# Who subtracts the attention's complement counts, and when their products run: one change to a graph network kernel on one core

## What is computed

```python
x = (meta_x @ W).reshape(N, HEADS, DIM)
a_src = jnp.sum(x * att_src, axis=-1)
a_dst = jnp.sum(x * att_dst, axis=-1)
logits = a_src[src] + a_dst[dst]
logits = jax.nn.leaky_relu(logits, NEG_SLOPE)        # slope 0.2
seg_max = jax.ops.segment_max(logits, dst, num_segments=N)
ex = jnp.exp(logits - seg_max[dst])
seg_sum = jax.ops.segment_sum(ex, dst, num_segments=N)
alpha = ex / (seg_sum[dst] + 1e-16)
msg = x[src] * alpha[:, :, None]
out = jax.ops.segment_sum(msg, dst, num_segments=N)
return out.mean(axis=1) + bias
```

## Time and profile before

| | |
|---|---|
| median of 3 runs | 1313.79 us (1310.27 to 1314.24) |
| the profiled execution | 1312.94 us, of which the span from first to last instruction is 1311.0 us |
| granted clock, mean of the span | 0.884 |
| busy over the span | PE 1171.5 us (89%), PEld 1106.4 (84%), DVE 884.3 (67%), ACT 624.2 (48%), POOL 63.0 (5%) |
| the 20 attention blocks, first nadS copy to last eviction | 855 us to 1303 us |

### The profile page before, as it was taken

One profiled execution on the slowest core, in us unless ns is written; L12 is line 12 of the kernel. 1 busy time (PEld: TensorE's weight loads), 2 busy tenths in 40 slices (PEclk: granted clock), 3 DMA queues, 4 the chain that ended last, 5 costly groups with the idle time before them and its releaser, 6 DMA issues.

```text
span 1311.0 us, 41073 instructions
## 1 busy us (share of the span) xinstructions
PE 1171.5 (89%) x17195; PEld 1106.4 (84%) x17195; DVE 884.3 (67%) x2404; ACT 624.2 (48%) x1143; POOL 63.0 (5%) x113
## 2 busy tenths in 40 slices
PE   0688888888999999999998699499999999999996
PEld 0588888888999999999986699488888888887996
DVE  1899999996443443443732723679778878887887
ACT  0566666662000000000112101478788888888886
POOL 2000000001111111111000001000000000000000
PEclk9855555558999999999999699699999999999998
DMA  1544444430000000000000000000000000000000
GB/s 27 83 70 60 63 65 68 63 58 11 3 3 2 3 2 2 3 2 2 3 2 2 1 2 2 1 2 1 2 1 2 2 1 2 2 2 1 7 12 12
DMA packets 133692, 21.47 MB, mean 16 GB/s; under 512 B 132961, under 2 KB 133378, under 8 KB 133538
## 3 DMA queue, kind: packets, MB, share of 16 engines
q1 hardware_dynamic: 132190, 18.75, 9.6%
q10 hardware_dynamic: 1252, 0.31, 0.1%
q0 software_dynamic: 96, 0.16, 0.1%
HBM read 18.41 MB, written 0.80 MB: 15 GB/s over the span
## 4 chain that ended last, share of the span: by engine, by line
PE 66%; DVE 17%; ACT 9%; issue 5%; DMA 1%; SPq 1%; POOL 0%; ACTq 0%; DVEq 0%; POOLq 0%
PE bank L1655 34%; PE bank L1781 11%; PE bank L1566 7%; PE bank L1777 5%; ACT Mr L852 4%; DVE Mr L1427 3%; PE bank L1569 3%; DVE ohk L941 2%; DVE ohp L943 2%; DVE Mr L1434 1%; ACT eahl L675 1%; PE bank L1570 1%; PE bank L1772 1%; ACT F L815 1%; DVE F L1326 1%
## 5 line engine op out<-in xcount | busy, mean ns | idle before, releaser
L1655 PEld LDWEIGHTS bank<-GH,C 128*128 128x128 f16 x8025 | 451.6, 98 | 8.3 <-issue 5.1
L1655 PE MATMUL bank<-GH,C 128*128 128x128 f16 x8025 | 453.7, 220 | 4.3 <-DVE GH L995 4.3
L1781 PE MATMUL bank<-F,Mr 128*128 128x260 f16 (+1 forms) x2520 | 343.7, 268 | 7.6 <-DVE Mr L1427 4.0
L852 ACT ACTIVATE Mr<-eaT 128x640 f16<-128x640 f32 x433 | 326.6, 822 | 30.1 <-PE bank L1781 28.1
L1781 PEld LDWEIGHTS bank<-F,Mr 128*128 128x128 f16 x2520 | 218.8, 98 | 31.1 <-DVE Mr L1427 4.7
L1427 DVE TENSOR_TENSOR Mr<-Mr,C 128x640 f16<-128x640 f16 x433 | 195.7, 488 | 72.7 <-ACT Mr L852 71.0
L725 ACT ACTIVATE plo<-bank 128x256 f32<-128x256 f32 (+1 forms) x91 | 32.8, 360 | 400.2 <-PE bank L1655 389.9
L1777 PE MATMUL bank<-FN,C 128*128 128x130 f16 x2260 | 209.8, 220 | 0.9 <-DVE r L1335 0.9
L1100 DVE TENSOR_TENSOR S<-bank,plo 128x256 f32<-128x256 f32 (+1 forms) x91 | 36.0, 395 | 246.9 <-ACT plo L725 246.9
L1566 PE MATMUL bank<-ohk,ohp 128*128 128x100 f16 (+3 forms) x1452 | 168.7, 281 | 10.8 <-DVE ohp L943 10.3
L1777 PEld LDWEIGHTS bank<-FN,C 128*128 128x128 f16 x2260 | 164.1, 98 | 10.5 <-DVE r L1335 1.4
(11 more groups left out here) (229 smaller groups left out, 834.7 us busy)
## 6 DMA issues: line engine op xcount, KB each, us to landing
raw<-in_edges_dram SPq DMA_DIRECT2D x242, 68.0 KB, 2.1
xs<-in_x_dram SPq DMA_DIRECT2D x1, 800.0 KB, 4.5
out_dram<-xs SPq DMA_DIRECT2D x4, 160.0 KB
wg<-in_L_gnn_W_dram ACTq DMA_DIRECT2D x2, 64.0 KB
z<-in_L_gnn_att_src_dram SPq DMA_DIRECT2D x1, 128.0 KB, 2.9
z<-in_L_gnn_att_dst_dram SPq DMA_DIRECT2D x1, 128.0 KB, 3.9
out_dram<-xs SPq DMA_DIRECT2D x1, 128.0 KB
wts<-in_L_gnn_W_dram ACTq DMA_DIRECT2D x3, 16.0 KB
```

Source lines behind the costliest of these rows:

```text
L852: act.activation(Mr[:, mi % RB, :], nadS, ACT.Sigmoid, bias=steep[:, h, t:t + 1], scale=-STEEP / XS).then_inc(s_step, 1)
L1655: last = pe.matmul(bank[:, b, jj * 2 * D:(jj + 1) * 2 * D], C[:, t, (t0 + jj) * P:(t0 + jj + 1) * P], GH[:, par, t, :], start=t == 0 and j ...
L1781: return pe.matmul(bank[:, k, a_:z_], Mr[:, mi % RB, j * P:(j + 1) * P], F[:, t, a_:z_], start=start, stop=t == T - 1)
```

## The change

The rule `apart` now takes the units 0, 4, 8, 12, 16 and 20 of blocks 1, 2 and 3, in all four heads: 72 units. Before it took these six in blocks 1 and 2 and four (0, 7, 14, 21) in block 3, in the first three heads: 48 units. GpSimd forms all complements, in a stream of its own that waits for the mask (`s_M`) and for the buffer (`s_Nu`). VectorE's `complement` is gone. PE takes the products of a complement after the masked products three units later, not one.

```diff
-            return h < H - 1 and (b in (1, 2) and t % 4 == 0 and t < T - 1 or b == 3 and t % 7 == 0)
+            return b in (1, 2, 3) and t % 4 == 0 and t < T - 1
...
-            with pool.If(dense3 == 0):
+            with pool.If(dense3 == 1):
+
+                for (h, b, t), ni in APART.items():
+                    pool.wait_ge(s_M, unit(h, b, t) + 1)
+                    if ni >= RN:
+                        pool.wait_ge(s_Nu, ni - RN + 1)
+                    pool.tensor_tensor(Nr[:, ni % RN], Mr[:, unit(h, b, t) % RB, :], C[:, t, b * NT * P:(b + 1) * NT * P], ALU.subtract).then_inc(s_N, 1)
+            with pool.Else():
...
-                            if t and apart(h, b, t - 1):
-                                complement(h, b, t - 1)
...
-                            if t and apart(h, b, t - 1):
-                                ni = APART[h, b, t - 1]
+                            if t >= 3 and apart(h, b, t - 3):
+                                ni = APART[h, b, t - 3]
                                 pe.wait_ge(s_N, ni + 1)
                                 for j in range(NT):
-                                    last = pe.matmul(bank[:, BANKS[b][j], 2 * S1:4 * S1], Nr[:, ni % RN, j * P:(j + 1) * P], F[:, t - 1, 2 * S1:4 * S1], start=False, stop=False)
+                                    last = pe.matmul(bank[:, BANKS[b][j], 2 * S1:4 * S1], Nr[:, ni % RN, j * P:(j + 1) * P], F[:, t - 3, 2 * S1:4 * S1], start=False, stop=False)
```

More of the change, by code:

```diff
@@ L1381, in final @@
                         last.then_inc(s_fin, 1)
[L1383 to L1389, removed]
                 scaled(0, 0)
```

## The result

The changed kernel takes 1366.43 us (median of 4 runs, 1361.57 to 1368.66) against 1313.76 for the kernel before: ratio 1.0402, 95% interval 1.0367 to 1.0436. It is 52.7 us slower; 1370 was forecast, inside 1316 to 1440. The profiled execution took 1368.66 us, its span 1366.8, 55.8 us longer than before's.

The account below looks back on a forecast made before the run. PE and VectorE were taken as level in blocks 1 and 2 of the first three heads. GpSimd's exclusions add 30 us there, 11 in blocks 3, 17 in the last head: + 58 on 1312.94, forecast 1370 us, range 1316 to 1440.

Parts of the forecast that it names:

- What bounds the kernel: Blocks 1 and 2 of the first three heads: PE and VectorE level, about 0.4 us of VectorE slack a block.
- the slack: VectorE's spare time in each of three last-head blocks, beyond its forced wait at the start: 1.0 us.
- What is removed: VectorE loses 48 complements of 0.40 us, 19 us in all; PE loses 6.7 us, 5.0 of them in the last head.
- rival 1: Faster: no exclusion between 16-bit masks and GpSimd, PE's 6.7 us gained; about 1306 us, 1302 to 1310; chance 0.13.
- The instruction's length: Each of 72 GpSimd complements of 640 16-bit elements takes 1.52 us, scaled by elements from 32-bit rows.
- The exclusion: GpSimd's complements and VectorE's two-tile masks exclude each other in full, costing VectorE 1.3 us each.
- rival 2: GpSimd goes by bytes, 0.85 us an instruction, one exclusion 0.65 us; + 13, 1326 us; chance 0.10.
- The new waits: PE's wait for a complement three units on should be free; ScalarE's wait for `s_N` is covered by 1.6 us of masks.
- a sign that it was wrong: In the changed profile, VectorE waiting for sigmoids in the middle of blocks would speak for starved GpSimd.
- Work under which GpSimd hides: GpSimd runs 1.5 us under two `scaled` in each block 3, and 1.0 us under pieces of `final` in last-head blocks.
- rival 3: GpSimd gets in only when masks run out; VectorE stands 2.2 us, not 1.3, 72 times; 1435 us; chance 0.10.
- rival 4: The clock falls as PE gets gaps of about 1.3 us; + 170, 1540 us; chance 0.05.

Follow-up runs that it names:

- the fills: Changed kernel with GpSimd filling the buffer twice in place of each complement: 1319.92 us; with a second complement buffer as well, 1310.48 us.
- the two runs that differ only in the engine: Changed kernel with a second complement buffer, once with VectorE forming all 72 complements, 1317.63 us, once with GpSimd forming them, 1360.76 us.
- the run with the engine alone: Kernel before, with GpSimd instead of VectorE forming its 48 complements; same units, products one unit behind, one buffer: 1343.10 us, ratio 1.0226.

## Why the prediction was right, point by point

- **What bounds the kernel**: right for blocks 1 to 3 of the first heads; two engines were level, and VectorE's time reached the end. For the last head the slack was wrong. I took 21.59 - 18.08 - 2.5 = 1.0 us for VectorE; six complements of 0.40 us on VectorE cost 1.9 to 2.1 of their 2.4 us there, so it was 0.3 to 0.5. The trace of before shows where the 1.0 us went. Its waits between 1234.06 and 1255.65 (total, times, longest) are:

```profile
DVE Mr L1427 <- ACT Mr L852: 3.1, 4, 2.4
```

  That is 0.6 us more than the 2.5 that I took off, for the second, third and fourth mask, and the 0.4 us that are left are, in VectorE's timeline, gaps of some 0.03 us between the small instructions of `post` and `final`, each of which waits for the one before. Idle time counted in a block is not all free.
- **What is removed**: right. 0.40 us each on VectorE. PE's 6.7 us came to nothing, as said, since PE was no longer the bound. But with the stops taken away (the fills, two buffers) the last head still didn't give PE's 1.7 us a block, as VectorE was level with PE there too, so rival 1 at 1306 was too low even if its mechanism had held: the fills ended at 1310 with two buffers and at 1320 with one.
- **The instruction's length**: 1.52 us forecast, 1.39 measured alone and 1.57 as the median, where it waits for a running mask. The error was small because the 32-bit rows carried over by elements; 0.60 us for 320 elements is 1.9 ns an element.
- **The exclusion**: right in kind. The 16-bit pair, which no row had shown, excludes like the others, so rival 1 is out, and so is rival 2, by the instruction's length. By the forecast's own rule, 1.39 - 0.28 + 0.08 = 1.19 us, and the two runs that differ only in the engine give 1.18. The forecast's 1.3 was too high by the length's error, 0.11 x 72 = 8 us.
- **The new waits**: this step of the prediction failed. I held GpSimd's wait for the buffer and ScalarE's wait for the complement to be covered. The second buffer gives 5.7 us in the changed kernel, and 9.4 where fills replace complements. The order of events is in the timeline of head 1, block 2, after:

```profile
1047.39 2.53 POOL L636 TENSOR_TENSOR Nr<-Mr,C 128x640 f16<-128x640 f16 x1 [2.29 <-PE bank L1839]
...
1050.87 1.45 DVE L1426 TENSOR_TENSOR Mr<-Mr,C 128x640 f16<-128x640 f16 x1 [2.21 <-ACT Mr L859]
```

  The complement could start only when PE had used the last one, met running masks and took 2.53 us; ScalarE stood for it, and VectorE 2.21 us for ScalarE, in the middle of a block, which the prediction had named as a sign that it was wrong. More than half of this loss goes with the later products (3.2 us in the six blocks 1 and 2, by the run with the engine alone). That the sum came out within 4 us is in part luck, as errors of opposite sign met: the exclusion too long (8 us too much), the last head's complements of unit 20 (next point, some 4 us too much), against the new waits (6 us), the last head's slack and cover, both taken too high (some 3 us together), and blocks 4 (0.8 us).
- **Work under which GpSimd hides**: right for the two `scaled` in block 3, which ran beside it at full speed; blocks 3 came to + 3.3 each where 3.6 was forecast. In the last head the small instructions were mostly not the cover I took them for. The five aggregations ran beside complement 8 at full speed, 0.43 us in all; the others stood too, as in this part of block 2 of the last head:

```profile
1292.57 0.43 DVE L1368 BATCH_NORM_AGGREGATE mv<-small 128x2 f32<-128x6 f32 x5
1293.04 0.89 DVE L1370 TENSOR_SCALAR eaT<-mv 128x5 f32<-128x5 f32 x1
...
1296.71 1.38 DVE L1381 SCALAR_TENSOR_TENSOR eaT<-eaT 128x5 f32<-128x5 f32 x1
```

  The last two take 0.17 us when left alone, on five elements. The first of these two reads a single tile. The Trainium skill (SBUF — State Buffer, § Who interferes with whom) names `tensor_scalar` among the instructions that may take both port pairs, and the trace agrees, with 0.89 us. I had held it for free. Even so the last head came out at + 13.9 us where 17 was forecast, and its slack was smaller than forecast. What covers there is the end of the block (GpSimd's row, then VectorE's):

```profile
1305.10 1.72 POOL L636 TENSOR_TENSOR Nr<-Mr,C 128x640 f16<-128x640 f16 x1 [3.23 <-PE bank L1839]
...
1303.08 2.49 DVE L1426 TENSOR_TENSOR Mr<-Mr,C 128x640 f16<-128x640 f16 x6
1307.98 0.49 DVE L1426 TENSOR_TENSOR Mr<-Mr,C 128x640 f16<-128x640 f16 x1 [2.41 <-ACT Mr L859]
```

  The complement of unit 20 came when only the block's last masks were left, let them pass at full speed (six in 2.49 us) and ran in the 2.41 us that VectorE has to wait anyway. In all three blocks it stopped no mask; five complements of six cost something.
- **Starved GpSimd (rival 3)**: not as a rule. 66 of the 72 complements last 1.39 to 1.73 us, so GpSimd got in at once or after the instruction that was running. Five last 2.12 us, having missed one turn more, and one, above, 2.53: it was passed over while three masks ran back to back (1047.38, 1.28 us in all). With two buffers, three last 2.78 or 2.79 us, behind four masks each (unit 20 of the last head's blocks, at the block's end, where it cost nothing). That is the rival in single places. Why GpSimd was let in elsewhere and not there stays open.
- **The clock (rival 4)**: a small part of it was there. After the long waits at the end of a block it fell for some 3 us. Busy time and clock at the end of head 1, block 1, after:

```profile
1024.00:1026.00 2.00, 0.22 (x4) 0.04 (x1) 2.00 (x2) 0.53 (x1) 1.58 (x1) 1.00 0.00 0
1026.00:1028.00 2.00, 1.28 (x11) 0.97 (x12) 0.67 (x2) 0.52 (x1) 0.00 (x0) 0.95 0.00 0
1028.00:1030.00 2.00, 2.00 (x14) 1.55 (x12) 0.70 (x2) 1.97 (x4) 0.00 (x0) 0.50 0.00 0
1030.00:1032.00 2.00, 2.00 (x18) 1.72 (x17) 0.78 (x2) 0.48 (x1) 0.47 (x1) 0.69 0.00 0
```

  PE had stood for 2.50 us before the target terms, then worked at 1.2 GHz from 1028 on, and was back at 2.4 GHz by 1032. Five of the nine blocks 1 to 3 of the first heads have a mean clock of 0.93 to 0.97. The two longest of the nine, 26.84 and 26.22 us, are among them, and so is the shortest, 25.16, so the clock doesn't set a block's length by itself. With two buffers the clock stays at 1.00 throughout, so of the 5.7 us that the second buffer gives some may be the clock's; the runs don't part the two.

## What to carry to other kernels

Before work goes to an idle engine, look for a place in the trace where that engine and the busy one run side by side on the kinds of operands in question, and compare each with itself alone; here four rows gave the price of an exclusion to 0.1 us before anything was run. An engine with free time is free only where the other one is kept from working by something else, as in the 2.4 us at a block's start: there 20 complements stopped no mask, where 72 in the stream cost 53 us, and with two buffers still 43 us more than the same 72 on VectorE. A single buffer between three engines makes each one's delay the next one's wait, and should be followed round the whole ring before it is called covered.

## What the runs showed of the hardware that was not expected

- GpSimd's fills read nothing and leave two-tile mask instructions alone (487 ns), but a single-tile one of VectorE on five elements took 0.61 us instead of 0.17 beside a fill. The view is the timeline of a block of the last head, in the run with fills and two buffers:

```profile
1241.01 0.63 POOL L640 MEMSET Nr<- 128x640 f16 x1
...
1241.06 0.61 DVE L1374 TENSOR_SCALAR eaT<-mv 128x5 f32<-128x5 f32 x1
```

- A copy of 640 16-bit elements on GpSimd takes 0.72 us, a fill 0.63, a subtraction of two tiles 1.39, and of half as many columns 0.79.
- The size of the VectorE instruction doesn't matter for how long it stands: one of five elements stood 1.2 us beside a complement, as long as a mask of 640. Instructions that read PSUM and one tile (0.82 us for `scaled`) and the aggregations (0.43 us for five) did not stand.
